# FFN products whose 512 columns are walked in two halves in turn

## The reference

```python
xn = _layernorm(x)                                   # x: (16, 512, 256)
# attention branch: linear attention with 16 heads, phi(x) = elu(x) + 1
q, k, v = split(xn @ W_qkv.T + b_qkv); q, k = phi(q), phi(k)
kv = k^T v ; k1 = sum(k) ; out = (q kv) / clip(q k1, 1e-6)
out = layernorm(out @ W_proj.T + b_proj) * gamma + beta + xn
# FFN branch: weights are -1, 0 or 1, each output has a float32 scale s
h = silu((xn @ w1.T) * s1) * ((xn @ w2.T) * s2)      # 256 -> 1024
h = gelu((h @ h1.T) * sh1)                           # 1024 -> 1024
h = gelu((h @ h2.T) * sh2)                           # 1024 -> 1024
y = (h @ w3.T) * s3                                  # 1024 -> 256
return x + out + y
```

## Time and profile before

| | us |
|---|---|
| median of 3 runs | 1606.58 (1605.88 to 1607.11) |
| span of the profiled execution, first to last instruction | 1605.2 |
| PE busy | 1591.0 (99%) |
| DVE busy | 945.4 (59%) |
| ACT busy | 527.6 (33%) |
| mean granted TensorE clock | 0.997 |

### The profile page before, as it was taken

How to read it: one execution, slowest core, us unless ns; L and a number is a source line. 1 busy time by engine, 2 the same in 40 slices (tenths; PEclk the granted TensorE clock), 3 DMA queues, 4 the chain that set the end, 5 groups by cost and what they waited for, 6 DMA issues and landing times.

```text
span 1605.2 us, 22443 instructions
## 1 busy us (share of the span) xinstructions
PE 1591.0 (99%) x7884; PEld 1326.0 (83%) x7884; DVE 945.4 (59%) x1927; ACT 527.6 (33%) x817; POOL 38.1 (2%) x44
## 2 busy tenths in 40 slices
PE   8999999999999999999999999999999999999998
PEld 5888888888888888888888888888888888888886
DVE  5656657466564656647566474664746646566563
ACT  3324142241423424233242332423324143241421
POOL 1000000000000000000000000000000000000000
PEclk9999999999999999999999999999999999999999
DMA  9000000000000000000000000000000000000000
GB/s 355 23 12 11 27 18 22 11 11 27 18 22 18 4 27 18 22 22 0 27 18 27 18 9 18 18 27 18 18 9 18 27 18 22 11 11 27 18 10 20
DMA packets 28114, 42.07 MB, mean 26 GB/s; under 512 B 2112, under 2 KB 26816, under 8 KB 27328
## 3 DMA queue, kind: packets, MB, share of 16 engines
q1 hardware_dynamic: 26800, 29.12, 5.7%
q0 software_dynamic: 864, 11.53, 1.8%
q10 hardware_dynamic: 432, 1.18, 0.2%
HBM read 33.44 MB, written 8.39 MB: 26 GB/s over the span
## 4 chain that ended last, share of the span: by engine, by line
PE 99%; DMA 0%; DVE 0%; POOL 0%; issue 0%; DVEq 0%; POOLq 0%
PE ps L386 74%; PE ps L519 7%; PE ps L391 4%; PE ps L392 4%; PE ps L393 4%; PE ps L442 2%; PE ps L431 2%; PE ps L452 1%; PE ps L401 1%; DMA x<-in_H 0%; DVE wqkv_parts L850 0%; DVE xn L714 0%; DVE bn_stats L708 0%; POOL rstd L353 0%; DVE xn L837 0%
## 5 line engine op out<-in xcount | busy, mean ns | idle before, releaser
L386 PE MATMUL ps<-hidden_a,w_ffn 128*128 128x512 f32 x2048 | 488.1, 397 | 0.0
L386 PE MATMUL ps<-hidden_b,w_ffn 128*128 128x512 f32 x2048 | 484.4, 396 | 0.0
L386 PEld LDWEIGHTS ps<-hidden_b,w_ffn 128*128 128x128 f32 x2048 | 383.5, 188 | 91.6
L386 PEld LDWEIGHTS ps<-hidden_a,w_ffn 128*128 128x128 f32 x2048 | 381.4, 188 | 88.5
L622 ACT ACTIVATE value_ring<-ps,vectors 128x512 f32<-128x512 f32 x256 | 173.1, 689 | 693.7 <-PE ps L386 684.4
L386 PE MATMUL ps<-xnT,w_ffn 128*128 128x512 f32 x1024 | 249.4, 398 | 0.0
L386 PEld LDWEIGHTS ps<-xnT,w_ffn 128*128 128x128 f32 x1024 | 190.1, 188 | 43.6
L803 DVE CAST hidden_a<-value_ring 128x512 fp32r<-128x512 f32 x128 | 54.5, 426 | 216.0 <-ACT value_ring L622 216.0
L789 DVE SCALAR_TENSOR_TENSOR value_ring<-ps,vectors,gate_ring 128x512 f32<-128x512 f32 x128 | 94.2, 746 | 83.5 <-ACT gate_ring L604 83.5
L519 PEld LDWEIGHTS ps<-w_ffn,hidden_a 128*128 128x128 f32 x1024 | 123.9, 188 | 2.9
L519 PE MATMUL ps<-w_ffn,hidden_a 128*128 128x256 f32 x1024 | 124.6, 279 | 0.0
(11 more groups left out here) (76 smaller groups left out, 1338.8 us busy)
## 6 DMA issues: line engine op xcount, KB each, us to landing
raw_weights<-in_w_ffn SPq DMA_DIRECT2D x64, 176.0 KB, 2.3
w_ffn<-in_w_ffn POOLq DMA_DIRECT2D x5, 2048.0 KB, 14.0
x<-in_H SPq DMA_DIRECT2D x16, 512.0 KB, 3.6
out_dram<-acc SPq DMA_DIRECT2D x32, 256.0 KB, 2.2
w_ffn<-in_w_ffn POOLq DMA_DIRECT2D x1, 1024.0 KB, 24.6
wqkv_raw<-in_w_attn ACTq DMA_DIRECT2D x1, 768.0 KB, 5.5
row_vectors<-in_rows SPq DMA_DIRECT2D x1, 512.0 KB, 7.8
wproj_raw<-in_w_attn ACTq DMA_DIRECT2D x1, 256.0 KB, 6.8
```

The costliest lines, as they stand in the source:

```text
L386: r = mm(bank, a, b, start=first and part == 0, stop=last and part == 1)
```

## The change

The 512 columns of the moving operand and of the output of each matmul at L386 are visited in another order: `run` columns of the first half (tokens 0 to 255), `run` of the second half (256 to 511), the next `run` of the first half, and so on. Both patterns change alike, so every result lands where it did. `run` is 2 in the gate stage, 4 in the first hidden stage and 8 in the second. `three`, `out_group` and all other engines are as before.

```diff
-            def products(bank, weight, act, first, last, full):
+            def halves_in_turn(ap, run):
+
+                return ap.rearrange("p (h n e) -> p n h e", h=2, e=run)
+
+            def products(bank, weight, act, first, last, full, run):
 
                 for part in range(2):
                     a, b = (weight, act(part)) if not full else (weight, f(act(part)))
-                    r = mm(bank, a, b, start=first and part == 0, stop=last and part == 1)
+                    r = mm(halves_in_turn(bank, run), a, halves_in_turn(b, run), start=first and part == 0,
+                           stop=last and part == 1)
                 return r
...
                             r = products(pair_bank(o, j), wt[:, base + k * HID + o * P:base + k * HID + (o + 1) * P],
-                                         lambda part: xnT[:, k, part, :], k == 0, k == DC - 1, full)
+                                         lambda part: xnT[:, k, part, :], k == 0, k == DC - 1, full, 2)
...
                         return products(pair_bank(g, j), wt[:, base + k * HID + o * P:base + k * HID + (o + 1) * P],
-                                        lambda part: src[:, k, part, :], k == 0, k == HC - 1, full)
+                                        lambda part: src[:, k, part, :], k == 0, k == HC - 1, full, (4, 8)[stage])
```

## The result

The changed kernel takes 1762.64 us (median of 4 runs, 1762.19 to 1763.08) against 1606.84 us (4 runs): a ratio of 1.0974, 95% interval 1.0961 to 1.0987. It is slower, as forecast, but by 155.8 us and not by 239.

The account below looks back on a forecast made before the run. TensorE, busy 1591.0 of 1605.2 us, was taken as the bound. Gate stage +238.9 us and hidden stages 0 gave a span of 1844.1, plus 1.4 for the median: 1845.5 us; range 1530 to 1885 us.

Parts of the forecast that it names:

- its case: Gate stage: reading cost doubles with runs of 2, hidden stages unchanged; forecast 1845.5 us, chance 0.45.
- the wide range: Whole kernel: 1530 to 1885 us, leaving out only the rival of jump costs in all stages and some edges.
- Both terms of the sum: L386 products: gate stage +238.9 us, hidden stages 0, added to the span of 1605.2 us.
- TensorE's own time goes to the end, nothing covers it: Whole loop: TensorE waits for nobody in the 16 tiles, so a product's gain or loss reaches the end one for one.
- A visit to a piece costs about 1.8 ns, however little is used: Reading operands: each visit to a 16-byte piece costs 1.8 to 2.0 ns on three engines; TensorE's stream pays 1.82.
- The term of the gate stage, 256 visits x 1.82 = 467 ns: Gate stage, runs of 2: 256 visits instead of 128, +233.3 ns a product, +238.9 us over 1024 products.
- the case of both kept: Gate stage: both halves of a piece served while kept at hand, adding 0; as rival no change, 1606.6 us, chance 0.17.
- The hidden stages, 4096 x 0: Hidden stages: runs of 4 or 8 are whole pieces, 128 visits as now, so 0 added over 4096 products.
- the sign that the prediction had named for a cost of the jump itself: Tile chain, 128-product piece of both hidden stages: longer than 29.87 us, or its halves differing, means jumps cost by themselves.
- Each jump costs because the written side must follow: Rival, all L386 stages: 655,360 jumps x 0.855 ns = +560 us, 2167 us; chance 0.12.
- Turns could hide what makes 0.456 of 0.427: Rival, L386 reading: halves in different memory slices save 14.6 ns a product, -75 us, 1532 us; faster side's chance 0.16.

Follow-up runs that it names:

- e3: Against the kernel before, only reading changed: gate halves in runs of 1, first hidden quarters in runs of 2, second hidden runs of 2 at 16 bytes' distance; 2475.5 us.
- g3: Against the kernel before, only reading changed: gate eighths in runs of 1, first hidden each column twice, second hidden every fourth column; 2304.0 us.
- f4: Against the kernel before, only reading changed: gate quarters in runs of 4, first hidden halves in runs of 16, second hidden halves in runs of 64; 1653.0 us.
- f3: Against the kernel before, only reading changed: second walk begins at column 254 (gate runs of 2, first hidden runs of 1) or 252 (second hidden runs of 4); 1690.7 us.
- e2: Against the changed kernel: only the output walked in turns (2, 4, 8), moving operand read in plain order; 1606.25 us, ratio 1.000 to the kernel before.
- e1: Against the changed kernel: only the moving operand walked in turns (2, 4, 8), output written in plain order; 1762.03 us, ratio 1.0969 to the kernel before.
- e4: Against the kernel before, reading repeated columns: gate one 16-byte piece, first hidden two pieces in turn, second hidden the same 2 columns; 1521.3 us.
- f1: Against the kernel before: all FFN products read halves in runs of 1, output plain, ScalarE and VectorE put tokens back; 1517.32 us, ratio 0.9449.

## Why the prediction was right in direction and off in size

The measured 1762.64 us lies outside the prediction's own range for its case (1838 to 1885 us). It lies inside the wide range (1530 to 1885 us), but that one spans nearly all rivals and says little. Both terms of the sum were off, the gate stage by -142 us and the hidden stages by +59 us; that they cancel in part and leave an error of only 83 us is luck.

1. *TensorE's own time goes to the end, nothing covers it.* Right: three waits, the other products unchanged, 155.7 us in the pieces against 156.1 in the span.
2. *A visit to a piece costs about 1.8 ns, however little is used.* Right where every visit fetches: 1.74 and 1.77 ns in e3, 1.80 in g3.
3. *The term of the gate stage, 256 visits x 1.82 = 467 ns.* Mis-sized: 327.5 measured, +96 us and not +239. The step that failed is the count of 256 full fetches, with no return that finds its piece kept. The prediction named the case of both kept, as its lower bound of 0, and took every return at full price; the truth lies between. e3's quarters, where the reader must go round four pieces, give 447, near the 467 that I had taken for the halves. Why the halves stop at 327 is argued, not shown.
4. *The hidden stages, 4096 x 0.* Mis-sized: +19.8 ns a product in runs of 4 and +8.9 in runs of 8, 0.15 and 0.14 ns a jump, together +59 us. It is the sign that the prediction had named for a cost of the jump itself. I counted visits alone and took the nearest row, the plain walk; f4 shows that the number of walks matters too, and f3 points to the distance. What a jump waits for stays open.
5. *Each jump costs because the written side must follow.* The place was wrong: e2 shows 0 for the writing. A jump price exists on the reading side (e1), at about a sixth of the 0.855 ns that this rival gave.
6. *Turns could hide what makes 0.456 of 0.427.* Right for runs of 1, which the change doesn't contain, and wrong for its runs. I held it against this rival that VectorE and ScalarE pay in full for 128-byte steps. The argument didn't carry over to TensorE, whose walk in runs of 1 gained. Nor do the halves have to lie in different slices of memory: 0 4 1 5 at 16 bytes' distance gains as much, and 0 2 1 3 within one piece nothing. What fits both is the split of the walk over two paths.

What the experiments show of the mechanism: the time of a 512-column product goes with the new 16-byte pieces that the even places and the odd places of the walk need, each for itself. 64 a path cost nothing (215.8 ns), 128 in sequence cost 17.5 ns, 256 give 447 to 462 ns. These sizes fit one picture, an estimate from these runs: a product takes 215.8 ns for its columns or 1.74 to 1.82 ns for each new piece of a path, whichever is longer (233.3 / 128 = 1.82, 446.6 / 256 = 1.74). The jumps in runs of 4 and 8 (253 and 242 ns) aren't in this picture, and a walk to and fro between two pieces doesn't fit it. It takes 217 ns with no new pieces a path (e4), 277 with 64 (f2) and 327 with 128 (the change), some 0.9 ns more for each new piece, as if added to the columns and not hidden behind them. That is three points and no mechanism. Two points stay open: why pieces that a path visits to and fro cost more than the same number in sequence (halves in runs of 2: 327; quarters in runs of 1: 277), and why more walks in turn are dearer at equal counts (266 against 253; 493 against 447). That a path keeps two pieces fits that the halves and quarters stay under 447, but not their sizes; this was not settled.

## What to carry to other kernels

When a product is bound by how its moving operand is read, change only the order of reading and only the order of writing, in separate kernels: here one had the whole cost and the other none. Where fp32r products fill TensorE, as here, let even and odd columns of the walk come from different halves, and let the engine that empties the bank put the values back; 6.7% came from that. And a price per visit taken from other engines held on TensorE only where every visit fetched (447 to 462 ns); for a walk that comes back to its pieces (327 ns) it was a guess.

## What the runs showed of the hardware that I had not expected

- A plain fp32r product of 512 columns isn't at the best rate seen here: 233.3 ns, where 215.8 is reached with the same clock (0.996 in f1, 0.997 before).
- Alternating between two walks at every column is the cheapest order (215.8), at every second column the dearest of the two halves in turn (327), and then it falls again (253, 242, 240, 233 for runs of 4, 8, 16, 64).
- The Trainium skill (Advanced Engine Details and Errata, Memory Cachelines) has that a 16-byte line needs at least two hits to absorb the access latency. If hits are counted by places of one path, the plain walk has exactly two hits a piece and loses 17.5 ns; four hits a piece (0 4 1 5) lose nothing; one hit about doubles the time (447 to 462 ns). So two hits are needed and not quite enough here.
